# float32r parts for keys, values and attention output, and the second layer norm on GpSimd

## The reference

```python
def _ln_t(v, eps=1e-05):
    m = jnp.mean(v, axis=-1, keepdims=True)
    s = jnp.var(v, axis=-1, keepdims=True)
    return (v - m) / jnp.sqrt(s + eps)
...
    t = _to_tokens(x)
    t = t + _L1_attn_ref(_ln_t(t), L1_attn_qkv_w, L1_attn_qkv_b, L1_attn_proj_w, L1_attn_proj_b, L1_attn_lambda_k1, L1_attn_lambda_v1, L1_attn_lambda_k2, L1_attn_lambda_v2)
    t = t + _L1_ffn_ref(_ln_t(t), L1_ffn_W1, L1_ffn_b1, L1_ffn_W2, L1_ffn_b2)
```

## Time and profile before

| what | us |
|---|---|
| median of 3 runs | 830.62 |
| lowest and highest of the runs | 829.88 and 832.27 |
| span of the profiled execution | 829.6 |
| TensorE matmul busy in it | 769.0 (93%) |
| VectorE busy | 636.5 (77%) |
| ScalarE busy | 476.7 (57%) |
| GpSimd busy | 180.2 (22%) |

### The profile page before, as it was taken

How to read it: one execution, slowest core, us unless ns; L and a number is a source line. 1 busy time by engine, 2 the same in 40 slices (tenths; PEclk the granted TensorE clock), 3 DMA queues, 4 the chain that set the end, 5 groups by cost and what they waited for, 6 DMA issues and landing times.

```text
span 829.6 us, 15136 instructions
## 1 busy us (share of the span) xinstructions
PE 769.0 (93%) x4663; PEld 510.4 (62%) x4663; DVE 636.5 (77%) x1945; ACT 476.7 (57%) x684; POOL 180.2 (22%) x209
## 2 busy tenths in 40 slices
PE   6798899999999999999999999999999999999991
PEld 3465566667666667666666766666766555555540
DVE  3576377877888878788877778887778468999997
ACT  2554445545555554545554555554553499988981
POOL 1440222332223232223232223233222000000000
PEclk8899989999999999999999999999999999999996
DMA  9950011101101101111110101010100101463333
GB/s 217 207 138 16 16 30 30 46 29 29 44 29 29 44 29 29 44 29 29 42 31 29 43 30 29 29 43 29 30 28 15 32 28 53 147 179 113 119 117 116
DMA packets 20351, 48.62 MB, mean 59 GB/s; under 512 B 4937, under 2 KB 5223, under 8 KB 20327
## 3 DMA queue, kind: packets, MB, share of 16 engines
q1 hardware_dynamic: 19928, 47.72, 21.0%
q10 hardware_dynamic: 399, 0.60, 0.3%
HBM read 29.51 MB, written 18.67 MB: 58 GB/s over the span
## 4 chain that ended last, share of the span: by engine, by line
PE 68%; DVE 11%; ACT 8%; issue 7%; SPq 3%; POOL 2%; DMA 1%; ACTq 0%; DVEq 0%; POOLq 0%
PE slot L1010 15%; PE slot L994 9%; PE slot L1017 7%; PE slot L1020 6%; PE slot L1158 6%; PE slot L1055 5%; PE slot L1187 5%; PE slot L1218 4%; PE slot L1222 4%; PE slot L862 4%; DVE stage L1470 4%; ACT stage L759 3%; SPq L442 3%; ACT hT L752 2%; PE slot L926 1%
## 5 line engine op out<-in xcount | busy, mean ns | idle before, releaser
L1436 DVE TENSOR_SCALAR tok<-tok,ln_mv,ln_rs 112x96 f32<-112x96 f32 x434 | 109.2, 322 | 58.2 <-POOL ln_rs L603 58.2
L1010 PE MATMUL slot<-hT,w2s 128*96 128x392 f32 x384 | 135.5, 503 | 3.0 <-ACT hT L752 2.3
L759 ACT ACTIVATE stage<-slot,minus_one 112x768 f32<-112x768 f32 x64 | 52.6, 822 | 125.6 <-PE slot L1055 123.3
L752 ACT ACTIVATE hT<-slot,b1c,w_unit 128x784 f32<-128x784 f32 x96 | 93.1, 1006 | 23.0 <-PE slot L994 23.0
L1010 PEld LDWEIGHTS slot<-hT,w2s 128*96 128x96 f32 x384 | 60.6, 164 | 64.1 <-issue 54.4
L603 POOL TENSOR_TENSOR ln_rs<-ln_ve,pow_half 112x7 f32<-112x7 f32 x62 | 91.8, 1481 | 4.8
L1017 PE MATMUL slot<-big,W1b 99*128 (+1 forms) x360 | 90.3, 332 | 2.1 <-ACT hT L816 0.6
L1020 PE MATMUL slot<-big,W1b 96*128 (+1 forms) x360 | 89.8, 330 | 0.0
L816 ACT ACTIVATE hT<-slot,s 128x784 f32<-128x784 f32 x90 | 80.3, 926 | 6.6 <-DVE stage L1554 6.3
L1442 DVE TENSOR_REDUCE ymax<-slot 128x784 f32 (+1 forms) x90 | 81.1, 956 | 0.1
L600 POOL TENSOR_TENSOR ln_ve<-ln_mv,ln_eps 112x7 f32<-112x7 f32 x62 | 12.5, 202 | 316.2 <-DVE ln_mv L1430 316.2
(11 more groups left out here) (190 smaller groups left out, 1285.2 us busy)
## 6 DMA issues: line engine op xcount, KB each, us to landing
out<-t2T SPq DMA_DIRECT2D x56, 294.0 KB, 2.6
xs<-in_x SPq DMA_DIRECT2D x32, 294.0 KB, 2.8
big<-in_x SPq DMA_DIRECT2D x7, 1176.0 KB, 15.3
xs<-out SPq DMA_DIRECT2D x24, 294.0 KB, 3.3
big<-out SPq DMA_DIRECT2D x1, 1764.0 KB, 11.6
out<-big SPq DMA_DIRECT2D x6, 294.0 KB, 2.6
big<-in_x SPq DMA_DIRECT2D x2, 588.0 KB, 24.1
con<-shape_consts ACTq DMA_DIRECT2D x1, 445.5 KB, 6.3
```

Of the source, the lines that this page charges most:

```text
L752: nc.scalar.activation(hT[:, t, :].rearrange("p (a n) -> p a n", a=2), halves(t, P), ACT.Relu, scale=w1_unit[:, t:t + 1], bias=b1c[:, t:t ...
L1010: ins = mm(S[k][0:C, h, 0:HALF], w2s[:, v, t, :], hT[:, t, h * HALF:(h + 1) * HALF], start=t == 0, stop=t == TILES - 1, skip_group_check=True)
L1436: ins = V.tensor_scalar(dst[:, j, :], src[:, j, :], ln_mv[n][:, j, 0:1], ln_rs[n][:, j:j + 1], ALU.subtract, ALU.mult)
```

## The change

It changes four things.

- The transposed tokens are kept as two tiles of type float32r, xh_hi and xh_lo. ScalarE's copy L777 writes xh_hi; VectorE subtracts it from PSUM for xh_lo, in the place in its order where `apply(1)` stood, and `kv` waits for this instead of for the copy. The keys' and values' weights are split likewise in the setup, and each product of `kv` becomes three (high x high, high x low, low x high).
- R is kept in two parts: ScalarE's copy L795 writes R_hi, VectorE subtracts for R_lo between the statistics of tok1 and the three maxima, and the attention output waits for R_lo. Each of its two products becomes three.
- The second norm's normalization goes from VectorE to GpSimd, as seven instructions (tokens plus negated mean, times the power), after a negation of the means put between L600 and L603. GpSimd's order is then: the low part of the coming image, L600, negation, L603, seven normalizations, and the first norm's L600 and L603.
- One memset of a one-partition row is added to the constants that all engines wait for at the start.

```diff
+                if n == 1:
+                    nc.gpsimd.tensor_scalar(ln_nm[:, :], ln_mv[n][:, :, 0], -1.0, None,
+                                            ALU.mult).then_inc(ln2_negated, 1)
...
+            def normalize_2(b):
+                wait_apart(pool, ln_rstd[1], b + 1, pool_passed)
+                wait_apart(pool, ln2_negated, b + 1, pool_passed)
+                for j in range(CHUNKS):
+                    ins = nc.gpsimd.tensor_scalar(tok2[:, j, :], tok2[:, j, :], ln_nm[:, j:j + 1],
+                                                  ln_rs[1][:, j:j + 1], ALU.add, ALU.mult)
+                ins.then_inc(xh2_ready, 1)
...
                     rstd(1, i - 2)
+                    normalize_2(i - 2)
                 rstd(0, i)
...
-                    nc.scalar.copy(*channels(xh1T[0:C, :], 0)).then_inc(xh1T_ready, 1)
+                    nc.scalar.copy(*channels(xh_hi[0:C, :], 0)).then_inc(xh1T_ready, 1)
...
-                    nc.scalar.copy(R[:, :], S[3][0:C + 1, 0, 0:C]).then_inc(r_ready, 1)
+                    nc.scalar.copy(R_hi[:, :], S[3][0:C + 1, 0, 0:C]).then_inc(r_ready, 1)
...
-                        ins = mm(chunks(k, n, 256, 2 * C)[:, j, :], xh1T[:, (j0 + j) * TOK:(j0 + j + 1) * TOK],
-                                 qkvw[:, C:3 * C], start=True, stop=True, skip_group_check=True)
+                        cols = slice((j0 + j) * TOK, (j0 + j + 1) * TOK)
+                        for p, (x_part, w) in enumerate(((xh_hi, kvw_hi), (xh_hi, kvw_lo), (xh_lo, kvw_hi))):
+                            ins = mm(chunks(k, n, 256, 2 * C)[:, j, :], x_part[:, cols], w[:, :],
+                                     start=p == 0, stop=p == 2, skip_group_check=True)
...
-                    pe.wait_ge(xh1T_ready, i)
+                    pe.wait_ge(xh_lo_ready, i)
...
-                    pe.wait_ge(r_ready, i)
-                    for h in range(2):
-                        ins = mm(S[3][0:C, h, 0:HALF], R[:, :], xh1T[:, h * HALF:(h + 1) * HALF],
-                                 start=True, stop=True, skip_group_check=True)
+                    pe.wait_ge(r_lo_ready, i)
+                    for p, (w, x_part) in enumerate(((R_hi, xh_hi), (R_hi, xh_lo), (R_lo, xh_hi))):
+                        for h in range(2):
+                            ins = mm(S[3][0:C, h, 0:HALF], w[:, :], x_part[:, h * HALF:(h + 1) * HALF],
+                                     start=p == 0, stop=p == 2, skip_group_check=True)
...
-            V.tensor_scalar(qkvw[C:C + 1, C:3 * C], qkvw[C:C + 1, C:3 * C], 1.0, None, ALU.add)
+            link(V.tensor_scalar(qkvw[C:C + 1, C:3 * C], qkvw[C:C + 1, C:3 * C], 1.0, None, ALU.add))
+            link(V.tensor_copy(kvw_hi[:, :], qkvw[:, C:3 * C]))
+            V.tensor_tensor(kvw_lo[:, :], qkvw[:, C:3 * C], kvw_hi[:, :].bitcast(F32), ALU.subtract).then_inc(kvw_ready, 1)
...
-                if ffn:
-                    apply(1, tok2, tok2, f, xh2_ready)
+                if attend:
+                    dve.wait_ge(xh1T_ready, i)
+                    V.tensor_tensor(tokenwise(xh_lo[0:C, :]),
+                                    flat(0)[0:C, 0:CHUNKS * P].rearrange("p (j t) -> p j t", t=P)[:, :, 0:TOK],
+                                    tokenwise(xh_hi[0:C, :].bitcast(F32)), ALU.subtract).then_inc(xh_lo_ready, 1)
...
                     stats(0, tok1, 1 if isinstance(i, int) and i == 0 else 2 * i)
+                if attend:
+                    dve.wait_ge(r_ready, i)
+                    V.tensor_tensor(R_lo[:, :], S[3][0:C + 1, 0, 0:C], R_hi[:, :].bitcast(F32),
+                                    ALU.subtract).then_inc(r_lo_ready, 1)
```

More of the change, by code:

```diff
@@ L13 @@
 BF16 = mybir.dt.bfloat16
+F32R = mybir.dt.float32r
 I32 = mybir.dt.int32
@@ L170, in build @@
         qkvw = sb("qkvw", [C + 1, 3 * C])
+        kvw_hi = sb("kvw_hi", [C + 1, 2 * C], F32R)
+        kvw_lo = sb("kvw_lo", [C + 1, 2 * C], F32R)
         wqT = sb("wqT", [C, C + 1])
@@ L247, in build @@
         ln_rs = [sb(f"ln_rs{n}", [TOK, CHUNKS]) for n in range(2)]
+        ln_nm = sb("ln_nm", [TOK, CHUNKS])
         w0_image = sb("w0_image", [TOK, CHUNKS])
@@ L250, in build @@
         tok2 = sb("tok2", [TOK, CHUNKS, C])
-        xh1T = sb("xh1T", [C + 1, HW])
+        xh_hi = sb("xh_hi", [C + 1, HW], F32R)
+        xh_lo = sb("xh_lo", [C + 1, HW], F32R)
         ekv = stage[0:TOK, 0:CHUNKS * 2 * C].rearrange("p (j c) -> p j c", c=2 * C)
@@ L256, in build @@
         St = sb("St", [C, C + 1])
-        R = sb("R", [C + 1, C])
+        R_hi = sb("R_hi", [C + 1, C], F32R)
+        R_lo = sb("R_lo", [C + 1, C], F32R)
         t2T = [sb(f"t2T{r}", [C, HW]) for r in range(2)]
@@ L287, in build @@
         dve_passed = sem("dve_passed")
+        pool_passed = sem("pool_passed")
         params_loaded = sem("params_loaded")
@@ L361, in build @@
         ln_rstd = [sem("ln1_rstd"), sem("ln2_rstd")]
+        ln2_negated = sem("ln2_negated")
         xh1_ready = sem("xh1_ready")
@@ L365, in build @@
         xh1T_ready = sem("xh1T_ready")
+        xh_lo_ready = sem("xh_lo_ready")
+        kvw_ready = sem("kvw_ready")
+        r_lo_ready = sem("r_lo_ready")
         kv_ready = sem("kv_ready")
@@ L421, in build @@
         N_PARAMS = 15
-        CONSTS_SET = (ones_ready, 10)
+        CONSTS_SET = (ones_ready, 11)
         def piece_of(b):
@@ L529, in _ @@
             nc.gpsimd.memset(two_ones[:, :], TWO_ONES).then_inc(ones_ready, 1)
-            pool.wait_ge(ones_ready, CONSTS_SET[1] - 2)
-            nc.gpsimd.memset(xh1T[C:C + 1, :], 1.0).then_inc(ones_ready, 1)
+            pool.wait_ge(ones_ready, CONSTS_SET[1] - 3)
+            nc.gpsimd.memset(xh_hi[C:C + 1, :].bitcast(F32), 1.0).then_inc(ones_ready, 1)
+            nc.gpsimd.memset(xh_lo[C:C + 1, :].bitcast(F32), 0.0).then_inc(ones_ready, 1)
             nc.gpsimd.memset(zg[:, :, :, :].rearrange("p a j w -> p (a j w)"), 0.0).then_inc(ones_ready, 1)
@@ L1036, in weights_flagged @@
                 pe.wait_ge(projb_loaded, 16)
+                pe.wait_ge(kvw_ready, 1)
                 pe.wait_ge(bigones_ready, 16)
```

## The result

The changed kernel takes 845.05 us (median of 4 runs, 843.85 to 848.21) against 831.1 before (median of 4 runs taken beside them): a ratio of 1.017, 95% interval 1.0141 to 1.0199. The forecast was 835.1, the range 826 to 871, slower the likeliest. So the direction holds, but of 14 us only 4.5 were foreseen. The profiled spans are 842.1 and 829.6 us, 12.5 apart.

What follows compares the result with a forecast made beforehand. TensorE was taken as the bound, with VectorE a second one behind product A. Per step +0.40 - 0.30 = +0.10, 3.0 in 30 steps, plus 1.5 at the ends: span 829.6 becomes 834.1, median 835.1 us; range 826 to 871.

Steps and rivals of the forecast that it cites:

- the second bound: Behind product A, VectorE runs without a gap from the mask through the normalization, arriving together with TensorE, which waits for it.
- R_lo's wait: On VectorE between statistics and maxima: R_lo waits for ScalarE's copy of R; maxima 0.44 later, 0.40 us per step lost.
- the rival of the covered delay: R copied before the statistics end, or t2T's transposes having more slack: only the 0.30 gain counts, 823 us; chance 0.12.
- the keys' gain: First part of keys and values: twelve matmuls of 0.083 us replace eight of 0.162, gaining 0.30 us per step.
- GpSimd's cover: Second norm on GpSimd: seven instructions of 0.39 us, usable by TensorE at 439.91, last harmless moment 439.94; met by 0.03.
- GpSimd is late: GpSimd's seven instructions at 0.57 take 1.26 us more, delaying feed-forward tile, R and R_lo: 871 us; chance 0.28.
- xh_lo is hidden within the loop: VectorE's xh_lo, 0.97 us, is hidden by the mix, except in first and last attention: 0.73 each, 1.5 us.
- The attention output: On TensorE: four instructions, 1.32 us, become six of 0.166, 0.99; the saving ends waiting for t2T, so nothing counted.
- The sum: Per step +0.40 - 0.30 = +0.10, in 30 steps 3.0, with 1.5 at the ends 4.5 us.
- float32r is no cheaper: In keys, values and attention output, float32r costs as much per column as float32: near +2.0 per step, 893 us; chance 0.14.

Runs made afterwards that it cites:

- e1: The changed kernel without VectorE's R_lo, the third product of the attention output taking R_hi instead: 826.07 us, ratio to before 0.9936.
- e2: The changed kernel with VectorE writing a same-sized R_lo out of constants, so that it waits for nothing: 832.76 us, ratio to before 1.0011.
- e3: The changed kernel with the second norm applied by VectorE again, behind xh_lo, and no negation on GpSimd: 838.5 us, ratio to before 1.0071.
- e9: The changed kernel with the keys' and values' second and third product loading 48 of 112 token columns as weights: 846.56 us, ratio to before 1.0181.

## Why the prediction came out as it did

**Right: the second bound.** That VectorE and TensorE arrive together behind A, and that R_lo's wait there is paid by the transposes of t2T, is what e1 and e2 show. The term was put at 0.44 for the maxima; it measures 0.143 + 0.279 = 0.42. In e3, which has R_lo without GpSimd's lateness, VectorE waits 0.19 for R, within the 0.15 to 0.2 that was to show it. Taking R_lo away makes the kernel faster than before, as the rival of the covered delay (823) had it for that condition. That e1's 826.07 is so near is in part luck: the 823 rests on a gain of 0.30 at the keys, where e1 has 0.13 there and another 0.11 from A to the next mix (9.766 - 9.653). One reading was loose: VectorE's records behind the mask do have a gap, the 0.15 ahead of L1430, in which it waits for its own statistics; it lies ahead of R_lo's place and changes nothing.

**Mis-sized: the keys' gain.** The step "I take 0.083 ... and the weight load of 112 columns is hidden now under 0.162" failed. Twelve instructions take 12 x 0.0985 = 1.18 for 1.31, and the gain measures 0.128, not 0.30. The range had this (0.097, "a weight load that shows", 840). The Trainium skill, TensorE: Matmul & The Clock Gate, section LDWEIGHTS, has a load's time go with its columns and gives columns / 1.2 in ns; an estimate from that page, 112 / 1.2 = 93 ns, is near the 98.5 measured, and I had passed it over. By the same estimate 64 columns fewer save 53 ns; e9's load records fell by 51 (175 to 124), so the trace agrees there too, while the 89 between its matmuls is set by something else. The Trainium skill, FP8 and Floating Point Precision, section TensorE Precision Notes, has true FP32 take four passes, and the trace agrees: two instructions of 0.162 are four times 0.081. Float32r's 0.0985 is nearer to one such 0.081; whether it is the page's reduced mode no run shows.

**Mis-sized: GpSimd's cover.** The step "It is met, by 0.03" failed. Counted from the mix, which the prediction had 0.40 late at 433.84, the seven were to begin at 3.19, to end at 5.92, and TensorE to take them at 6.07, against a last moment of 6.10. They began at 407.98 - 404.66 = 3.32, ended at 6.15 and were taken at 6.21. The instruction was nearly right (0.402 from start to start, (2.83 - 0.42) / 6, for 0.39), and the negation and the waits ahead of it added 0.13. Being 0.11 late instead of 0.03 early cost 0.164 in each step, and, with the step of the gate's weights, whose later statistics the prediction had not looked at, 6.5 us by e3. This is the rival "GpSimd is late" in small. The Trainium skill's "roughly line-rate" (GPSIMD Engine Reference, section 4.1) does not show here: GpSimd takes 0.402 us from one instruction of 96 elements to the next, where VectorE takes 1.75 / 7 = 0.25.

**Right, and small.** xh_lo is hidden within the loop; only at the ends do the keys wait for it. The last attention after, against the earlier trace rows:

```profile
660.00 0.81 ACT L801 CAST xh_hi<-slot 96x784 fp32r<-96x784 f32 x1 [6.45 <-PE slot L886]
660.84 0.97 DVE L1513 TENSOR_TENSOR xh_lo<-slot,xh_hi 96x784 fp32r<-96x784 f32 x1 [1.65 <-ACT xh_hi L801]
...
661.86 0.35 PE L1082 MATMUL slot<-kvw_hi,xh_hi 97*112 97x192 f32 x1 [1.04 <-DVE xh_lo L1513]
```

From the copy to the keys 1.86 for 0.86: 1.00, less the keys' 0.13, makes 0.87 where 0.73 was put. The attention output fell from 1.32 to 418.06 - 416.90 = 1.16, not 0.99, and in the changed kernel gained nothing, as forecast, because t2T's transposes wait for VectorE (0.23 at 420.45).

**The sum.** Put: -0.30 + 0.40 = +0.10 per step and 1.5 at the ends. Measured: -0.128 + 0.483 = +0.355 (of the 0.586 at the maxima, 0.483 reach the mix), 1.3 once in the step with the gate's weights, and 0.87 at the last attention. The difference of 0.255 per step is made of 0.172 (the keys) and 0.164 (GpSimd), less 0.02 (R_lo) and 0.06 (more of the maxima's delay is lost on the way to the mix than the 0.04 put).

That 845 lies inside the range owes something to luck: the part of it above 842 was there for GpSimd instructions of up to 0.57, and they took 0.402. The time got there by the keys' smaller gain and the lateness together, which the prediction had only one at a time.

The rival "float32r is no cheaper" is out: 0.0985 an instruction, not 0.162. Its sum has a slip: an attention output 0.66 longer passes a delay of 0.40 by 0.26 and not by 0.4, which makes its 893 too high by some 4; nothing hangs on it.

## What to carry to other kernels

When a matmul gets cheaper by its columns, price what those columns had covered, its weight load first: here half the expected gain and more stayed there. A small operation that waits for a late value costs its wait on the engine whose queue it stands in (here 0.42 with the wait, 0.14 without), and another place in the queue may only move the wait to its reader. Two parts that are each nearly free (the norm on GpSimd +0.2%, the keys -0.8%) need not be so together, since one was covered by what the other shortened; change them one at a time.

## What the runs showed of the hardware

A float32r matmul of 192 columns took 0.0985 us with a load of 112 columns, as long on average with 128 moved columns, and some 0.089 with a load of 48; so the load of 112 columns sets the first two, and what sets the third is not shown. Two numbers were higher than expected beside it: 0.18 us for 392 columns in float32r ((417.69 - 417.33) / 2 between the pairs of the attention output), where float16 took 0.166, and GpSimd's 0.421 us for a tensor-scalar of 96 elements, a third of the 1.251 for 384.
